# One fused attention and projection kernel: its projection stage written out without loops, the two parts of x cut by ScalarE and VectorE, SyncE led by events, and in the attention stage the attended lower part cut by VectorE with the residual sums first

## The chip, the core and the metric

The kernel runs on one core of a Trainium2 chip. The metric is the device time of one execution in microseconds (us), as a median over runs. The core has five engines with a queue each: TensorE (PE) multiplies matrices, VectorE (DVE), ScalarE (ACT) and GpSimd (POOL) work on elements, and SyncE (SP) issues transfers (DMA). They meet only at semaphores. A wait in a queue holds everything behind it in that queue.

## The reference

x has 2 sequences of 2048 rows of 1024. One attention layer with 32 query heads of 32 and a single key and value head, a residual sum with a layer norm, one product with a 1024x1024 weight (both operands scaled and clipped to 448 and scaled back), a second residual sum and layer norm.

```python
q = (x @ wq_w.T + wq_b).reshape(b, t, H, HD)        # H = 32, HD = 32
k = (x @ wk_w.T + wk_b).reshape(b, t, HKV, HD)      # HKV = 1
v = (x @ wv_w.T + wv_b).reshape(b, t, HKV, HD)
scores = jnp.einsum('bqhd,bkd->bhqk', q, k1) / jnp.sqrt(jnp.float32(HD))
weights = jax.nn.softmax(jnp.where(causal, scores, -jnp.inf), axis=-1)
attn = jnp.einsum('bhqk,bkd->bqhd', weights, v1).reshape(b, t, H * HD)
x1 = _layernorm(x + attn @ wo_w.T + wo_b)
x_sim = jnp.clip(x1 * x_scale, -448, 448)
w_sim = jnp.clip(weight * w_scale, -448, 448)
out = _layernorm(x1 + x_sim @ w_sim * (1.0 / (x_scale * w_scale)))
```

## The kernel before, in words

Every queue is written out by hand; there is no scheduler. A value that needs precision is held as an upper part (a cast to fp32r) and a lower part (the value less the upper part), and a product is made of three matmuls: upper by upper, lower by upper, upper by lower (`THREE`).

**Projection stage.** x comes transposed in TB = 8 blocks of 512 rows. For each block PE makes MT = 9 tiles: G = 8 units of queries (`project`, 24 matmuls each, into two PSUM banks in turn) and one tile of keys and values (`project_keys`, 16 matmuls, one bank for all blocks). `norm` sums squares after the fifth unit and after the keys. In the last block the keys come first; PE waits there for `raw_ready` of the block before, that is until ACT has copied the keys of that block out of their bank. For a unit ACT adds the bias (`raw`) and squares it (`sq`), DVE cuts `raw` into `part_hi` and `part_lo` (`cut_queries`), ACT stores both (`send`). `raw` and the parts have two buffers, so unit m of PE waits for the squares of unit m-2, and those for DVE's cut of unit m-2 before. For the keys ACT copies one part of the bank (`kv_sum`, L756), DVE adds the other (L963), ACT makes four copies with the bias (L759, L760).

The parts of x: `xt_raw` has one buffer in two halves, `xt_hi` and `xt_lo` have two buffers. In block 0 ACT makes `xt_hi` and DVE `xt_lo` by halves. From block 1 on POOL does both in `cut_x` (L644 cast, L646 subtraction), and behind each half adds the output bias to two row tiles of x (`add_bias_row`, L633), 32 in all, which SP loads from x and stores to `xb_d`. The 9 tiles of the projection weight are cut by DVE (L928, L931) before its first `cut_queries`. DVE also measures, and in blocks 4 to 7 clips, the 8 tiles of the second weight (`wf_tile`).

SP's queue is a loop over blocks: load half of x, wait for its landing, two row loads, two row stores (each waits for POOL), then the weight tile. After the loop come the last two pairs of rows, then the loads of the output weight `w_o` into `xt_raw` (L452), which ACT (`upper_wo`, L784) and DVE (`lower_wo`) cut during the last block. In the last block ACT's queue has, per unit: `add_bias`, `send` of the unit before, `upper_wo` of the unit before, and in four units squares of keys. DVE reduces key norms there (L1015), for which PE's `key_norm` (L1288) waits.

**Attention stage.** 544 steps; a step is one key tile of 128 against 16 heads of a query tile. PE makes scores (L1365), ACT the exponential (L838), DVE adds it into `acc` (L1117; the first addition of a group has the line L1113), PE weighs the values (L1377). Groups of steps end with `denominators` (L1387), `invert` on DVE, `spread_out` on PE (L1395) and `normalise_group` on DVE. Finished query tiles are cut into `att_hi` (ACT, L825) and `att_lo` (POOL, L689), multiplied with the output weight between scores (`half_projection`, L1350), and DVE adds the residual (`add_residual`, L1094) and takes moments. At which step each of these stands is set by `places`: a tile is cut at its step 4 or 13, and its product begins at 6 or 22.

**Last stage.** Loops over 32 row tiles with the second product. Nothing of it is touched.

## Time and profile before

| what | us |
|---|---|
| median of 3 runs (2452.33 to 2453.8) | 2452.48 |
| the profiled execution: its own time | 2451.5 |
| its span, first to last instruction | 2449.8 |
| PE busy in the span | 2347.4 |
| DVE busy in the span | 1859.7 |
| ACT busy in the span | 1319.6 |
| POOL busy in the span | 918.0 |

The granted TensorE clock has a mean of 0.988 of full speed. PE's projection runs from 13.28 to 438.82 us of the span, attention from 444.10. The duration of a matmul in the trace is longer than the distance from one to the next, since they overlap: in the projection 0.39 us and 0.227 us at full clock.

### The profile page before, as it was taken

Reading aid. Unit: us, or ns where it says so; the run is one execution under the profiler, and the core shown is the slowest. Engines: PE = TensorE matmul, PEld = TensorE weight load, DVE = VectorE, ACT = ScalarE, POOL = GpSimd, SP = SyncE. Lnnn points to the kernel's source line nnn. Section 1 sums busy time; section 2 is a strip of 40 time slices with the busy share of each in tenths; the row PEclk is TensorE's granted clock in tenths of the full one; section 3 lists DMA queues with packets and bytes.
Section 4 is the critical chain, followed back from the end, with each engine's and each line's share of the span. In section 5 each row is a group of like instructions: output and inputs, shape, how many; then the busy total and the mean of one; then the engine's idle time right before and its main releaser. Section 6 shows DMA issues by size and latency. Waiting matters only on the chain.

```text
span 2449.8 us, 35663 instructions
## 1 busy us (share of the span) xinstructions
PE 2347.4 (96%) x13933; PEld 1488.8 (61%) x13933; DVE 1859.7 (76%) x1387; ACT 1319.6 (54%) x1443; POOL 918.0 (37%) x472
## 2 busy tenths in 40 slices
PE   6999998789999999999999999999999998999998
PEld 5778776335555555555555555555555556888887
DVE  6655665788888888888889998888888886444444
ACT  2232224577777777777777676777777773100000
POOL 2553453013233233234232323332324323666563
PEclk9999999899999999999999999999999999999999
DMA  7775767231222112212221122212221212222221
GB/s 234 260 254 204 278 241 258 60 62 36 53 57 66 44 45 66 66 45 58 53 66 44 44 55 63 58 44 61 53 63 44 66 61 112 91 89 86 86 94 61
DMA packets 159958, 231.55 MB, mean 95 GB/s; under 512 B 9582, under 2 KB 109902, under 8 KB 157774
## 3 DMA queue, kind: packets, MB, share of 16 engines
q1 hardware_dynamic: 136206, 178.27, 25.1%
q10 hardware_dynamic: 23616, 51.39, 5.5%
q8 instruction: 94, 1.54, 0.3%
q14 instruction: 42, 0.34, 0.1%
HBM read 140.50 MB, written 89.13 MB: 94 GB/s over the span
## 4 chain that ended last, share of the span: by engine, by line
PE 64%; DVE 7%; ACT 5%; POOL 3%; issue 2%; DMA 0%; ACTq 0%; DVEq 0%; POOLq 0%
PE bank L1365 18%; PE bank L1377 16%; PE bank L1440 14%; PE bank L1350 12%; ACT prob L838 4%; DVE acc L1117 4%; POOL att_lo L689 2%; PE bank L1387 2%; PE bank L1430 1%; DVE acc L1113 1%; PE bank L1395 1%; POOL prob L684 1%; DVE r_den L1077 1%; ACT att_hi L825 1%; DVE r_hi L1079 0%
## 5 line engine op out<-in xcount | busy, mean ns | idle before, releaser
L838 ACT ACTIVATE prob<-bank 128x1024 f32<-128x1024 f32 x1088 | 1055.4, 1023 | 422.5 <-PE bank L1365 394.7
L1117 DVE TENSOR_TENSOR acc<-acc,prob 128x2048 f32<-128x2048 f32 x420 | 987.4, 2351 | 71.4 <-ACT prob L838 48.6
L1365 PE MATMUL bank<-q_st,keys 98*128 98x512 f32 x2176 | 646.8, 416 | 16.5 <-ACT prob L838 13.3
L1365 PEld LDWEIGHTS bank<-q_st,keys 98*128 98x128 f32 x2176 | 376.5, 189 | 352.9 <-ACT prob L838 258.4
L1377 PE MATMUL bank<-prob,v_t 128*32 128x512 f32 x4352 | 526.2, 601 | 0.0
L684 POOL TENSOR_SCALAR_AFFINE_SELECT prob<-prob 128x1024 f32<-128x1024 f32 x128 | 204.1, 1617 | 591.6 <-ACT prob L838 591.6
L1377 PEld LDWEIGHTS bank<-prob,v_t 128*32 128x32 f32 x4352 | 114.0, 109 | 263.4 <-issue 251.9
L1113 DVE TENSOR_TENSOR acc<-prob 128x2048 f32<-128x2048 f32 x60 | 141.5, 2358 | 118.5 <-ACT prob L838 78.7
L1259 PE MATMUL bank<-xt_hi,w_hi 128*128 128x512 f32 x512 | 204.8, 400 | 19.1 <-DVE xt_lo L921 15.3
L1350 PE MATMUL bank<-wo_hi,att_hi 128*128 128x512 f32 x512 | 209.1, 408 | 11.9 <-POOL att_lo L689 8.5
L869 ACT ACTIVATE xs_hi<-bank 128x1024 fp32r<-128x1024 f32 x32 | 32.9, 1027 | 336.3 <-DVE y L900 261.5
L689 POOL TENSOR_TENSOR att_lo<-att,att_hi 128x1024 fp32r<-128x1024 f32 x31 | 99.7, 3217 | 295.9 <-ACT att_hi L825 295.9
L621 POOL TENSOR_SCALAR moments<-moments 128x1 f32<-128x1 f32 x64 | 68.6, 1072 | 367.9 <-DVE moments L895 361.1
L1350 PE MATMUL bank<-wo_hi,att_lo 128*128 128x512 f32 x512 | 202.8, 396 | 0.0
L1440 PE MATMUL bank<-wf_hi,xs_hi 128*128 128x512 f32 x512 | 202.2, 395 | 0.7 <-DVE xs_lo L1189 0.7
L1350 PE MATMUL bank<-wo_lo,att_hi 128*128 128x512 f32 x512 | 202.5, 396 | 0.0
L1259 PE MATMUL bank<-xt_lo,w_hi 128*128 128x512 f32 x512 | 202.3, 395 | 0.0
L1259 PE MATMUL bank<-xt_hi,w_lo 128*128 128x512 f32 x512 | 202.2, 395 | 0.0
L1440 PE MATMUL bank<-wf_lo,xs_hi 128*128 128x512 f32 x512 | 199.7, 390 | 0.0
L1440 PE MATMUL bank<-wf_hi,xs_lo 128*128 128x512 f32 x512 | 199.3, 389 | 0.0
L766 ACT ACTIVATE raw<-bank,bias 128x512 f32<-128x512 f32 x64 | 44.1, 689 | 252.8 <-PE bank L1259 226.7
L953 DVE CAST part_hi<-raw 128x512 fp32r<-128x512 f32 x64 | 86.3, 1349 | 104.4 <-ACT raw L766 70.1
(132 smaller groups left out, 2643.2 us busy)
## 6 DMA issues: line engine op xcount, KB each, us to landing
q_st<-q_hi_d SPq DMA_DIRECT2D x128, 256.0 KB
xt_raw<-x_t SPq DMA_DIRECT2D x16, 1024.0 KB, 6.6
q_hi_d<-part_hi ACTq DMA_DIRECT2D x64, 256.0 KB, 2.7
q_lo_d<-part_lo ACTq DMA_DIRECT2D x64, 256.0 KB, 3.2
x_row<-x SPq DMA_DIRECT2D x32, 512.0 KB, 4.6
xb_d<-x_row SPq DMA_DIRECT2D x32, 512.0 KB, 2.7
q_st<-q_lo_d SPq DMA_DIRECT2D x64, 256.0 KB
res<-xb_d SPq DMA_DIRECT2D x32, 512.0 KB, 5.7
```

Of the source, the lines that this page charges most:

```text
L621: nc.gpsimd.tensor_scalar(moments[:, 1:2], moments[:, 1:2], LN_EPS, None, ALU.add).then_inc(done, 1)
L684: nc.gpsimd.affine_select(out=tri, in_=tri, compare_op=ALU.is_ge, fill=0.0, base=0, pattern=[[0, 2 * HG], [1, P]], channel_multiplier=-1). ...
L689: nc.gpsimd.tensor_tensor(att_lo[q % 2][:], att[:, q % TILES_KEPT], att_hi[q % 2][:].bitcast(F32), ALU.subtract).then_inc(att_cut, 1)
L838: nc.scalar.activation(prob[:, s % SLOTS, 2 * p:2 * p + 2], bank[:, 2 * p:2 * p + 2], ACT.Exp, scale=SCALE).then_inc(p_done, 1)
L953: nc.vector.tensor_copy(part_hi[:, m % 2], raw[:, m % 2]).then_inc(hi_cut, 1)
L1113: nc.vector.tensor_tensor(acc[:, n % 2], prob[:, (s - 1) % SLOTS], new, ALU.add).then_inc(acc_done, 2)
L1117: nc.vector.tensor_tensor(acc[:, n % 2], acc[:, n % 2], new, ALU.add).then_inc(acc_done, 1)
L1259: last = nc.tensor.matmul(dst, (w_hi, w_lo)[a][:, m, k], (xt_hi[:, r], xt_lo[r])[c][:, k], start=(k == 0 and a == c == 0), stop=(k == KT - ...
L1350: last = nc.tensor.matmul(dst, (att_hi, att_lo)[a][q % 2][:, k], (wo_hi, wo_lo)[c][:, k, cols], start=(at == 0), stop=(at == len(todo) - 1 ...
L1365: last = nc.tensor.matmul(bank[:, g].rearrange("p (a n) -> p a n", n=P), keys[:, k // QT, k % QT * P:(k % QT + 1) * P], queries[:, :, g], ...
L1377: last = nc.tensor.matmul(bank[g * HD:(g + 1) * HD, 4 + n % 2], v_t[:, k // QT, k % QT], prob[:, s % SLOTS, g], start=(t == 0), stop=(t == ...
L1440: last = nc.tensor.matmul(bank[:, 4 + 2 * (r % 2) + h], (xs_hi, xs_lo)[a][:, r % 2, k], (wf_hi, wf_lo)[c][:, k, cols], start=(k == 0 and a ...
```

## The change

SP, POOL, ACT and DVE have the projection stage written out without loops, and in PE blocks 0 and 1 are outside the loop (as blocks 6 and 7 were). Three functions of the block and the unit say where a piece of side work stands: `half_at` (halves of x), `row_at_unit` (row tiles), `tile_use` (tiles of the second weight).

- x of block 0 comes in four quarters, issued without a wait between them, with a semaphore each; ACT and DVE cut quarters, and PE's first unit waits for quarters. The four stores of zeros by ACT come behind its four casts.
- x of block b+1 is cut during block b: ACT casts a half (`upper_x`, 128x2048) and DVE subtracts (`lower_x`), at units 1 and 4 (5 and 7 in block 0). POOL has none of it.
- DVE adds the bias to the row tiles, one tile at each of five units in blocks 1 to 6, two in block 7. POOL has none of it.
- DVE cuts four weight tiles ahead of its first `cut_queries` and one tile ahead of each of the next five.
- SP waits for the event that frees a buffer at the place where it comes in DVE's order, and issues the loads of `w_o` behind row 29, ahead of the stores of rows 30 and 31.
- In the attention stage DVE makes `att_lo`, and at a step that has several pieces the residual sums stand ahead of `invert`, `normalise_group` and `att_lo`; the moments behind.

```diff
@@ SP
-            for half in range(2):
-                sp.dma_start(xt_raw[:, k], x_t[0, :, k]).then_inc(xt_in, 16)
-                sp.wait_ge(xt_in, 16 * (half + 1))
+            for quarter in range(4):
+                k = slice(quarter * KT // 4, (quarter + 1) * KT // 4)
+                sp.dma_start(xt_raw[:, k], x_t[0, :, k]).then_inc(xt0_in[quarter], 16)
             for m in range(1, MT):
                 load_w(m)
+                if m == 6:
+                    load_x(1, 0)
+                    load_x(1, 1)
...
+            for b in range(TB - 1):
+                for m in range(G):
+                    if half_at(b, m) is not None and b + 2 < TB:
+                        load_x(b + 2, half_at(b, m))
+                    if row_at_unit(b, m) is not None:
+                        next_row(row_at_unit(b, m))
+                    if tile_use(b, m) is not None:
+                        next_tile(tile_use(b, m))
@@ POOL
-                    nc.gpsimd.tensor_copy(xt_hi[:, r, k], xt_raw[:, k]).then_inc(xt_hi_cut, 1)
-                    nc.gpsimd.tensor_tensor(xt_lo[r][:, k], xt_raw[:, k], xt_hi[:, r, k].bitcast(F32), ALU.subtract).then_inc(xt_cut, 1)
-                nc.gpsimd.tensor_tensor(x_row[:, i], x_row[:, i], bo[:], ALU.add).then_inc(x_row_added, 1)
-                    nc.gpsimd.tensor_tensor(att_lo[q % 2][:], att[:, q % TILES_KEPT], att_hi[q % 2][:].bitcast(F32), ALU.subtract).then_inc(att_cut, 1)
@@ ACT
+            for tb in range(TB - 1):
                 for m in range(MT):
                     add_bias(tb, m, m)
                     if m >= 1:
                         send(tb, m - 1)
+                    if half_at(tb, m + 1) is not None:
+                        upper_x(tb + 1, half_at(tb, m + 1))
@@ DVE, projection
+            for tb in range(TB - 1):
+                for m in range(G):
+                    if tb == 0 and m + 4 < MT:
+                        cut_weight(m + 4)
+                    cut_queries(tb, m, m)
...
+                if half_at(tb, m) is not None:
+                    lower_x(tb + 1, half_at(tb, m))
+                if row_at_unit(tb, m) is not None:
+                    add_bias_row(row_at_unit(tb, m))
@@ DVE, attention
+                if s in sum0_at:
+                    add_residual(sum0_at[s], 0)
+                if s in sum1_at:
+                    add_residual(sum1_at[s], 1)
                 if s % 2 == 0 and s // 2 in group_of_den:
                     invert(group_of_den[s // 2])
                 if s % 2 == 0 and s // 2 - 1 in group_of_den:
                     normalise_group(group_of_den[s // 2 - 1])
-                if s in sum0_at:
-                    add_residual(sum0_at[s], 0)
+                if s in split_at:
+                    lower_attended(split_at[s])
```

The DVE queue in block 0, before: the last two weight tiles, then the first queries.

```order
L928 CAST w_hi<-w_stage 128x1024
L931 TENSOR_TENSOR w_lo<-w_stage,w_hi 128x1024
L928 CAST w_hi<-w_stage 128x1024
L933 TENSOR_TENSOR w_hi<-w_stage,w_hi 128x8x64
L990 UNCONDITIONAL_BRANCH
L990 ISA
L952 ISA
L953 CAST part_hi<-raw 128x512
L954 ISA
L955 TENSOR_TENSOR part_lo<-raw,part_hi 128x512
```

The same queue now, behind weight tile 3.

```order
L903 CAST w_hi<-w_stage 128x1024
L906 TENSOR_TENSOR w_lo<-w_stage,w_hi 128x1024
L951 CAST part_hi<-raw 128x512
L953 TENSOR_TENSOR part_lo<-raw,part_hi 128x512
L903 CAST w_hi<-w_stage 128x1024
L906 TENSOR_TENSOR w_lo<-w_stage,w_hi 128x1024
L951 CAST part_hi<-raw 128x512
L953 TENSOR_TENSOR part_lo<-raw,part_hi 128x512
```

The cut of the first queries moved from behind nine weight tiles to behind five.

SP's queue at the end of the projection, before (the L405 and L408 rows are the last two pairs of row tiles, L452 is the output weight).

```order
L405 DMA x_row<-x 128x1024 x2
L408 DMA xb_d<-x_row 128x1024 x2
L405 DMA x_row<-x 128x1024 x2
L408 DMA xb_d<-x_row 128x1024 x2
L452 DMA xt_raw<-w_o 128x1024 x4
```

The same place now.

```order
L438 DMA xb_d<-x_row 128x1024
L433 DMA x_row<-x 128x1024
L438 DMA xb_d<-x_row 128x1024
L433 DMA x_row<-x 128x1024
L465 DMA xt_raw<-w_o 128x1024 x4
L438 DMA xb_d<-x_row 128x1024 x2
```

The loads of the output weight passed the stores of the last two rows, and rows 0 to 29 are done by the end of block 6.

DVE's queue at one of the steps 4 of the attention stage, before (L1087 is `normalise_group`).

```order
L1117 TENSOR_TENSOR acc<-acc,prob 128x2048 x2
L1087 TENSOR_TENSOR att<-att,bank 128x512
L1094 TENSOR_TENSOR res<-bank,res 128x512
L893 BN_STATS stats<-res 128x6 x2
L895 BN_AGGR moments<-stats 128x2
L1117 TENSOR_TENSOR acc<-acc,prob 128x2048 x7
```

The same step now.

```order
L1118 TENSOR_TENSOR acc<-acc,prob 128x2048 x2
L1090 TENSOR_TENSOR res<-bank,res 128x512
L1083 TENSOR_TENSOR att<-att,bank 128x512
L1100 TENSOR_TENSOR att_lo<-att,att_hi 128x1024
L876 BN_STATS stats<-res 128x6 x2
L878 BN_AGGR moments<-stats 128x2
L1118 TENSOR_TENSOR acc<-acc,prob 128x2048 x7
```

The residual sum passed the normalisation, and the lower part stands between it and the moments.

## Rows read from the trace of the kernel before

**Rows 1.** Page part 1: busy us (share of the span) and instructions by engine.

```profile
PE 2347.4 (96%) x13933; PEld 1488.8 (61%) x13933; DVE 1859.7 (76%) x1387; ACT 1319.6 (54%) x1443; POOL 918.0 (37%) x472
```

**Rows 2.** Windows of PE: stretch, length, PE busy (x), granted clock, DMA share, GB/s.

```profile
13.28:76.01 62.73, 54.06 (x217) 0.94 0.68 232
76.01:125.55 49.54, 49.54 (x217) 0.97 0.74 264
125.55:173.84 48.29, 48.29 (x217) 1.00 0.76 273
...
366.98:375.29 8.31, 0.00 (x1) 0.81 0.60 236
375.29:438.82 63.53, 57.54 (x256) 0.94 0.71 241
```

**Rows 3.** Timeline of the start: start, us, engine, line, what, [idle before <-releaser].

```profile
8.99 1.91 ACT L742 ACTIVATE xt_hi<-xt_raw 128x2048 fp32r<-128x2048 f32 x1 [3.48 <-DMA xt_raw<-x_t]
10.93 2.29 DVE L921 TENSOR_TENSOR xt_lo<-xt_raw,xt_hi 128x2048 fp32r<-128x2048 f32 x1 [3.26 <-ACT xt_hi L742]
...
13.28 0.79 PE L1259 MATMUL bank<-xt_hi,w_hi 128*128 128x512 f32 x1 [13.28 <-DVE xt_lo L921]
...
20.16 0.50 PE L1259 MATMUL bank<-xt_hi,w_hi 128*128 128x512 f32 x1 [2.04 <-DVE xt_lo L921]
...
44.95 0.80 PE L1259 MATMUL bank<-xt_hi,w_hi 128*128 128x512 f32 x1 [3.82 <-ACT sq L768]
...
75.39 0.62 PE L1236 MATMUL bank<-sq,head_sum 128*32 128x512 bf16 x4 [2.81 <-ACT sq L768]
```

**Rows 4.** Tile w_stage: from the issue of a 512 KB load to its landing.

```profile
DMA to landing us min/median/max: 3.4/3.8/4.7
```

**Rows 5.** Timeline at the end of block 6, POOL, DVE and PE.

```profile
360.40 4.66 POOL L646 TENSOR_TENSOR xt_lo<-xt_raw,xt_hi 128x2048 fp32r<-128x2048 f32 x1
...
360.63 4.98 DVE L955 TENSOR_TENSOR part_lo<-raw,part_hi 128x512 fp32r<-128x512 f32 x1
...
370.79 0.68 DVE L937 TENSOR_REDUCE norms<-bank 128x512 f32 x1
371.39 0.67 DVE L963 TENSOR_TENSOR kv_sum<-bank,kv_sum 64x512 f32<-64x512 f32 x1
...
375.29 3.75 PE L1245 MATMUL bank<-xt_hi,w_hi 128*128 128x512 f32 x8 [8.31 <-issue]
```

**Rows 6.** Timeline of the last block: SP, ACT and PE.

```profile
396.30 2.25 SPq L452 DMA_DIRECT2D xt_raw<-w_o  x4
...
401.42 1.06 ACT L784 ACTIVATE wo_hi<-xt_raw 128x1024 fp32r<-128x1024 f32 x1 [8.28 <-DMA xt_raw<-w_o]
...
414.11 0.37 PE L1288 MATMUL bank<-kv_sum,head_sum 32*32 32x512 bf16 x1 [2.07 <-DVE norms L1015]
...
428.84 0.37 PE L1288 MATMUL bank<-kv_sum,head_sum 32*32 32x512 bf16 x1 [1.91 <-DVE norms L1015]
```

**Rows 7.** Attention stage, windows: stretch, length, busy of PE, PEld, DVE, ACT, POOL.

```profile
480.00:1960.00 1480.00, 1442.35 (x9680) 785.54 (x9680) 1293.67 (x864) 1076.89 (x1137) 472.68 (x235) 1.00 0.22 54
```

**Rows 8.** Lines of PE from 480 to 1960 us: busy, mean ns | idle before, releasers.

```profile
L1350 PE MATMUL bank<-wo_hi,att_hi 128*128 128x512 f32 x456 | 186.7, 409 | 11.9 <-POOL att_lo L689 8.5 <-DVE res L1094 3.1
...
L1387 PE MATMUL bank<-acc,head_col 128*32 128x128 f32 x1952 | 65.9, 276 | 7.8 <-DVE acc L1117 7.8
...
L1395 PE MATMUL bank<-r_parts,spread 128*128 128x128 f32 x240 | 35.4, 270 | 9.3 <-DVE r_parts L1081 9.2
```

**Rows 9.** Tile att_lo: duration ns min/median/max, first and last start.

```profile
L689 POOL TENSOR_TENSOR att_lo<-att,att_hi x31: 2374/3542/4021, 553.9 to 2021.1; 128x1024 fp32r<-128x1024 f32 x31
L1143 DVE TENSOR_TENSOR att_lo<-att,att_hi x1: 1224/1224/1224, 2037.0 to 2037.0; 128x1024 fp32r<-128x1024 f32 x1
```

**Rows 10.** Tile acc (min/median/max ns), then page part 5 (busy us, mean ns).

```profile
L1117 DVE TENSOR_TENSOR acc<-acc,prob x420: 2266/2292/4297, 452.3 to 2028.1; 128x2048 f32<-128x2048 f32 x140
...
L1117 DVE TENSOR_TENSOR acc<-acc,prob 128x2048 f32<-128x2048 f32 x420 | 987.4, 2351 | 71.4 <-ACT prob L838 48.6
```

**Rows 11.** Timeline at one step 4 of the attention stage.

```profile
1047.52 3.54 POOL L689 TENSOR_TENSOR att_lo<-att,att_hi 128x1024 fp32r<-128x1024 f32 x1 [11.00 <-ACT att_hi L825]
...
1048.74 0.68 DVE L1087 TENSOR_TENSOR att<-att,bank 128x512 f32<-128x512 f32 x1
```

More of the change, by code:

```diff
@@ L191, in build @@
         zeros_sent = sem("zeros_sent")
-        xt_in = sem("xt_in")
+        xt0_in = [sem(f"xt0_in{i}") for i in range(4)]
+        xt0_hi, xt0_cut = sem("xt0_hi"), sem("xt0_cut")
+        xt_in = [sem("xt_in0"), sem("xt_in1")]
         xt_hi_cut, xt_cut = sem("xt_hi_cut"), sem("xt_cut")
@@ L437, in _, with load_row @@
-            load_x(KT // 2, 0)
-            load_tile(KT - 1)
-            load_x(KT // 2, 1)
-            sp.wait_ge(wf_tile_read, KT + 1)
-            sp.dma_start(wf_tile[:], w_f[:, 0]).then_inc(wf_tile_in, 16)
-            with sp.Fori(KT // 2 + 1, TB) as tb:
-                for half in range(2):
-                    load_x(tb, half)
-                    store_piece(tb * 2 + (half - 2 - KT))
-                    load_piece(tb * 2 + (half - 1 - KT))
-            for pair in range(TILES // 2 - 2, TILES // 2):
-                add_bias_rows(pair)
+            def load_row(r):
+                sp.dma_start(x_row[:, r % 2], x_tiles[r]).then_inc(x_row_in[r % 2], 16)
@@ L733, in _ @@
                 act.sem_inc(s, 16)
+            for quarter in range(4):
+                k = slice(quarter * KT // 4, (quarter + 1) * KT // 4)
+                act.wait_ge(xt0_in[quarter], 16)
+                nc.scalar.activation(flat(xt_hi[:, 0, k]), flat(xt_raw[:, k]), ACT.Copy).then_inc(xt0_hi, 1)
             act.wait_ge(consts, 5)
@@ L738, in _ @@
                     act.dma_start(max_d[c].rearrange("t h n -> (t h) n")[i * P:(i + 1) * P], zeros).then_inc(zeros_sent, 16)
-            for half in range(2):
-                k = slice(half * KT // 2, (half + 1) * KT // 2)
-                act.wait_ge(xt_in, 16 * (half + 1))
-                nc.scalar.activation(flat(xt_hi[:, 0, k]), flat(xt_raw[:, k]), ACT.Copy).then_inc(xt_hi_cut, 1)
             act.wait_ge(b_in, 16)
@@ L768, in add_bias, with upper_x @@
                     nc.scalar.activation(sq[:, m % HG], bank[:, m % 2], ACT.Square, bias=bias[:, m:m + 1]).then_inc(sq_ready, 1)
-            with act.Fori(0, TB - 1) as tb:
+            def upper_x(tb, half):
+                k = slice(half * KT // 2, (half + 1) * KT // 2)
+                act.wait_ge(xt_in[half], 16 * tb)
+                nc.scalar.activation(flat(xt_hi[:, tb % 2, k]), flat(xt_raw[:, k]), ACT.Copy).then_inc(xt_hi_cut, 1)
+            for tb in range(TB - 1):
                 for m in range(MT):
@@ L967, in sum_keys @@
                 nc.vector.reduce_sum(centre_part[0:SR, bass.ds(tb, 1)], one(kv[0:SR, bass.ds(tb, 1)]), AX.X).then_inc(k_summed, 1)
-            def block_work(tb, use_tile):
-                for m in range(G):
-                    cut_queries(tb, m, m, use_tile)
-                norm(tb, 1)
-                add_lower_keys(tb)
-                sum_keys(tb, G)
             def weight_scale():
@@ L1141, in _ @@
             lower_wf(0)
[L1142 to L1143 removed]
+            lower_attended(LAST_B)
             for i in range(1, 4):
@@ L1255, in project @@
                 for k in range(KT):
-                    if k % (KT // 2) == 0:
+                    if first and k % 2 == 0:
+                        pe.wait_ge(xt0_cut, k // 2 + 1)
+                    elif not first and k % (KT // 2) == 0:
                         pe.wait_ge(xt_cut, tb * 2 + (2 + k // (KT // 2) + 1))
@@ L1261, in project, with project_block @@
                 last.then_inc(qkv_done, 1)
-            def project_block(tb, r):
+            def project_block(tb, r, first=False):
                 for m in range(G):
-                    project(tb, r, m)
+                    project(tb, r, m, first and m == 0)
                     if m == HG:
@@ L1269, in project_block @@
                 norm(tb, 1)
-            with pe.Fori(0, TB // 2 - 1) as i:
+            project_block(0, 0, first=True)
+            project_block(1, 1)
+            with pe.Fori(1, TB // 2 - 1) as i:
                 for r in range(2):
```

167 lines of the change are left out of this document (74 added, 93 removed).

## The prediction, written before the changed kernel ran

> **What bounds the kernel now.** I read the busy shares first: PE is busy 96% of the span, DVE 76%, ACT 54%, POOL 37% [rows 1]. So a gain has to come from PE: from time in which it stands still, or runs at its lower clock, or starts late. Then I cut PE's projection into blocks. Blocks 2 to 6 take 48.29 us each and PE is busy in all of it (one of the five is in [rows 2]): there the projection has nothing to give, and the loops that end inside this stretch cost PE nothing. Block 0 takes 62.73 us with 54.06 busy, the last block 63.53 with 57.54 busy, and between blocks 6 and 7 PE stands for 8.31 us [rows 2]. The timeline of the start says why: the first matmul waits until 13.28 for the lower part of half of x, then come gaps of 2.04, 3.82 and 2.81 us [rows 3]. In the attention stage PE is busy 1442.35 of 1480 us, DVE 1293.67, which is 87% [rows 7]; PE's idle 37.7 us are all that stage can give, and any DVE work added there meets an engine that is nearly full. One unit of 24 matmuls is 24 x 0.227 = 5.44 us; a block is 8 of these, 16 matmuls of keys (3.6) and two norms.
>
> **The start.** Now the first half of x lands at 8.99, ACT casts it in 1.91 and DVE subtracts in 2.29 [rows 3]: 8.99 + 1.91 + 2.29, with some 0.1 between, is 13.28. With quarters, ACT takes 1.06 (the same shape in [rows 6]) and DVE 1.22 [rows 9]. When the first quarter lands is not in the trace. It cannot be before 1.7 + 3.4 = 5.1 (issue behind the first weight tile, and the fastest landing of 512 KB [rows 4]) nor after 8.99. I take 6.3: it is nearer to the lower end since the zeros, 1 MB that shared the DMA engines, now go later. PE starts at 6.3 + 1.06 + 1.22 = 8.6 (bounds 7.5 and 11.3). Gain 4.7 us (2.0 to 5.8).
>
> The quarters then follow each other at intervals that I estimate at 1.5 us (the engine steps are 1.06 and 1.22), while PE at half clock needs 6 x 0.45 = 2.7 us for a quarter, so the gap of 2.04 has no successor.
>
> **Blocks 0 and 1.** Block 0 lost 62.73 - 48.29 = 14.4 us: gaps 8.67, and 54.06 - 48.29 = 5.8 of matmuls at the lower level, 1.2 GHz (mean granted clock 0.94 [rows 2]); block 1 takes 49.54 and adds 1.3. These 7.1 us belong to four stretches, at the start and behind each gap: 1.8 us each. The 3.82 gap exists because DVE cuts all nine weight tiles before the first queries, so ACT has no free `raw`; the 2.81 gap because DVE's queries stood behind stretched operations beside POOL. After the change a weight tile is 0.69 + 1.23 of DVE work per unit of 5.44 us and is loaded at a rate of one per load and cut, at most 4.7 + 1.9 = 6.6 us for a buffer, two buffers, so 3.3 us a tile: faster than PE uses them. What is left is the low clock of the start itself, 1.8 us. Gain 14.4 + 1.3 - 1.8 = 13.9 us (bounds 8, if one of the later gaps survives with its clock loss, and 15.7).
>
> **What moves onto ACT and DVE.** 14 halves of x: ACT 14 x 1.91 = 27 us, DVE 14 x 2.29 = 32 us [rows 3]. 32 row tiles on DVE: this form is not in the trace for DVE; between 1.22 (same size, subtraction [rows 9]) and twice that, I take 1.22, so 39 us. Per unit DVE then has 1.1 for the queries, at most 2.29 or 1.22 + 1.5 beside, under 4.5 of 5.44 us: hidden behind PE. Cover goes if a row tile is not there when DVE waits for it, for the queries stand behind this wait, then ACT, then PE. A row's load follows the landing of the store two rows earlier, 2 x 4.7 us at most by [rows 4] against two units of 10.9 us; and `raw` has two buffers, which gives one more unit. I cost it at 0, with an upper bound of 5 us.
>
> **Between blocks 6 and 7.** PE waits for ACT's copies of the keys, and those for DVE's sum, which begins at 371.39, since its queries were stretched: a `part_lo` that takes 0.69 us elsewhere takes 4.98 beside POOL's subtraction of 4.66 [rows 5]. From the end of that sum to PE's start it is 375.29 - 372.06 = 3.2 us of ACT. With DVE free at 366.98 it needs 0.68 for the norm and 0.67 for the sum: 366.98 + 1.4 + 3.2 = 371.6, a gap of 4.6 us instead of 8.31. Gain 3.7 us (0 to 4.3). The clock drops all the same, as it did after 2.81 us.
>
> The Trainium skill, SBUF — State Buffer, "SBUF: two separate sides", says that VectorE and GpSimd share one port pair as an exclusive lock, and whoever comes second waits for the whole instruction of the other. The 4.98 us are 0.3 us more than POOL's own 4.66, so the trace agrees here.
>
> **The last block.** Against 8 x 5.44 + 3.6 and some 4.8 of norms, transposes and key norms, 51.9 us, it takes 63.5: 6.0 of gaps, 5.6 of low clock. The first cause is ACT: its queue stands 8.28 us on the output weight that SP issues only at 396.30, behind four row tiles [rows 6]. All units after it come late, DVE with them, and PE waits 2.07 and 1.91 for key norms. In the new order SP issues these loads behind row 29, about 20 us before ACT's first use of them, so they land (5 us, from 396.30 to 401.42) ahead of need. What is late next are the key norms themselves: DVE has about 5.0 to 6.3 us of work in units 3 to 6 against 5.44, so I leave 1.5 us of waits, and 1.8 of low clock behind the boundary gap: 55.2 us. Gain 8.3 us (3 to 9.8). At the end of the stage DVE comes out of unit 6 about 1 us late for the flag: loss 0.9.
>
> **Attention.** DVE gets 31 x 1.22 = 38 us [rows 9]. It loses what POOL did to it: the additions have a mean of 2351 against a median of 2292 ns, 420 x 0.059 = 25 us [rows 10], plus about 6 in other forms. The net is some +7 us on an engine with 186 us of idle, so the bound stays PE. On the path: at a step 4, POOL delivers at 1047.52 + 3.54 = 1051.06; DVE begins its side work at 1048.74 [rows 11] and has 0.6 + 0.6 + 1.22 ahead of the end of `att_lo`: 1051.2. Equal, so the 8.5 us of PE waiting for `att_lo` [rows 8] stay, under another name. At a step 13 the stretched addition (up to 4.3 instead of 2.3) is replaced by 1.22 us, so groups that end soon after are 0.4 to 0.8 us earlier: of the 7.8 us of waits for `acc` and the 9.3 for `r_parts` I take 5 back. Residual sums first: saves perhaps 1 of the 3.1 for `res`, and costs up to 0.6 at each of about 15 steps where `invert` now stands behind it; I charge 3. Net gain 3 us (bounds -10 and +12).
>
> The lock rule named above would make each of the 31 subtractions hold DVE for its full median 3.54 us, 110 us in all, and moving them would free 110 - 38 = 72 us of DVE. The additions show 25, so the rule alone overstates it here: at the steps 4 it is POOL that is stretched and DVE keeps its 2.29. The sum goes by the 25.
>
> **Sum.** 4.7 + 13.9 + 3.7 + 8.3 - 0.9 + 3 = 32.7 us, of which 29.7 before the attention stage. The profiled execution took 2451.5 (span 2449.8), so 2418.8; the median of the runs is 1.0 above it: 2420 us.
>
> **Rivals.** (a) Half of the projection's gain: new waits take the place of the old. For it: the DMA share is already 0.7 [rows 2], and SP's queue is now a chain of store, wait, load, so one late store delays x or `w_o`. Against it: x is loaded a block ahead. Then 2451.5 - 15 - 3 + 1 = 2434. (b) DVE in the attention stage becomes the bound, the slower side. Place: steps 4 of each pair, and denominators after a step 13. Price: if none of the 38 us are covered and nothing comes back from POOL, -29.7 + 38, 8 us more than now, so 2461; it decides from the point at which each of the 31 subtractions exposes more than 29.7 / 31 = 0.96 us on PE. For it 87% busy; against it that `prob` has four buffers (`SLOTS`), so ACT's exponential of a step needs the addition of four steps earlier, and a late one is not noticed at once. (c) Attention gives more: waits for `acc`, `r_parts` and `res` go by 12 us, not 3, and the start is at its early bound, 1 us more: 2410. (d) The change does not do what it says: PE's first unit waits for the fourth quarter in effect, or the boundary wait is unmoved since it hangs on ACT; then the first term or the third is zero, 2424 or 2425. This lies within my range.
>
> **How the numbers follow.** The forecast, with (d) inside, has 0.70 and its own range is 2412 to 2428. (a) has 0.14, (c) 0.12, (b) 0.04. The range of 2410 to 2434 holds the forecast, most of (c) and half of (a). Faster or slower begin at 0.2%, 5 us, about what a measurement of this kernel can tell from no change. All cases but (b) are faster; for what I have not thought of I leave a little: faster 0.93, within 3%, slower 4%.
>
> **What would show it.** First matmul between 7.5 and 11.3, block 0 under 51 us, and the later gaps of block 0 gone: the start is right. `part_lo` at 0.69 us throughout and a gap of 4 to 5 us ahead of the last block: the boundary. The output weight issued ahead of the last block, no ACT wait on it, and the last block at 54 to 57 us: the third term. In attention the additions at 2.3 us with waits for `att_lo` about as before. I am wrong if PE in blocks 1 to 6 is no longer busy throughout (a row tile or a half of x came late), or if the waits in the attention stage exceed 45 us.

## The result and the profile after

| | median us | lowest to highest | runs |
|---|---|---|---|
| before | 2452.40 | 2449.0 to 2453.8 | 4 |
| after | 2417.06 | 2413.82 to 2417.97 | 4 |

The ratio is 0.9853 with a 95% interval of 0.9835 to 0.9870: 35.3 us faster. The profiled execution of after has a span of 2411.7 us against 2449.8, so 38.1 us less, which is what the terms below are taken from. (It is the fastest of the four executions of after; the spans of the other three are 2414.3 to 2415.9.) PE's first score matmul starts at 417.83 instead of 444.10: 26.3 us come from the projection stage, 11.8 from behind it.

The busy times of the engines after, against [rows 1]:

```profile
PE 2338.3 (97%) x13933; PEld 1484.1 (62%) x13933; DVE 1809.0 (75%) x1466; ACT 1346.0 (56%) x1459; POOL 640.1 (27%) x381
```

POOL lost 278 us of work. ACT gained 26 for its 14 halves of x. DVE took over subtractions, row tiles and `att_lo` and is nevertheless 51 us less busy: what it had lost to stretching was more than what it was given. The clearest form is this one, which had a mean of 1349 ns before:

```profile
L951 DVE CAST part_hi<-raw 128x512 fp32r<-128x512 f32 x64 | 28.3, 443 | 140.6 <-ACT raw L741 121.7
```

PE's windows after, with the columns of [rows 2]: blocks 0 and 1, the gap ahead of the last block, the last block, and the tail up to the first scores.

```profile
9.23:59.32 50.09, 50.09 (x217) 1.00 0.78 288
59.32:107.60 48.28, 48.28 (x220) 1.00 0.71 250
349.04:353.57 4.53, 0.07 (x4) 0.72 0.60 172
353.57:411.20 57.63, 55.76 (x256) 0.96 0.66 228
411.20:417.83 6.63, 0.59 (x4) 0.60 0.29 108
```

Block 0 has no gap left and costs 1.8 us more than a full-speed block; blocks 1 and 2 are at the 48.29 that was the floor (48.28 and 48.29). The gap is 4.5 us instead of 8.3, the last block 57.6 instead of 63.5, still with 1.87 us idle inside: the waits for key norms are 0.5 us (4.4 before), and 1.4 us are one wait for ACT's squares, which before had too.

The start after (same columns as [rows 3]):

```profile
1.74 2.03 SPq L413 DMA_DIRECT2D xt_raw<-x_t  x4
...
6.70 1.06 ACT L713 ACTIVATE xt_hi<-xt_raw 128x1024 fp32r<-128x1024 f32 x1 [3.99 <-DMA xt_raw<-x_t]
7.79 2.54 DVE L914 TENSOR_TENSOR xt_lo<-xt_raw,xt_hi 128x1024 fp32r<-128x1024 f32 x2 [0.25 <-ACT xt_hi L713]
...
9.23 0.77 PE L1264 MATMUL bank<-xt_hi,w_hi 128*128 128x512 f32 x1 [9.23 <-DVE xt_lo L914]
```

And the end of block 6, against [rows 5]: the lower part takes 0.69 us (4.98 before), the norm and the sum of the keys follow the bank at once, and the wait of PE is ACT's 3 us of copies with little ahead of them. SP issues the output weight at 357.31 (396.30 in [rows 6]).

```profile
346.34 0.69 DVE L953 TENSOR_TENSOR part_lo<-raw,part_hi 128x512 fp32r<-128x512 f32 x1
...
349.16 0.69 DVE L935 TENSOR_REDUCE norms<-bank 128x1 f32<-128x512 f32 x1 [0.99 <-PE bank L1239]
...
350.47 2.21 ACT L734 ACTIVATE kv<-kv_sum,bias 32x512 f32<-32x512 f32 x3 [1.07 <-DVE kv_sum L965]
...
353.57 3.75 PE L1248 MATMUL bank<-xt_hi,w_hi 128*128 128x512 f32 x8 [4.47 <-issue]
357.31 2.01 SPq L465 DMA_DIRECT2D xt_raw<-w_o  x4
```

In the attention stage, first the window with the columns of [rows 7]; it begins the same distance behind the first scores as the window of before did:

```profile
453.70:1933.70 1480.00, 1452.90 (x9744) 791.69 (x9744) 1302.27 (x900) 1085.36 (x1146) 378.49 (x206) 1.00 0.22 55
```

PE is idle for 27.1 us of it, not 37.7. PE's lines from 453 to 1933 us, against [rows 8], show which waits went:

```profile
L1357 PE MATMUL bank<-wo_hi,att_hi 128*128 128x512 f32 x462 | 189.0, 409 | 14.4 <-issue 11.3 <-DVE res L1090 3.1
...
L1394 PE MATMUL bank<-acc,head_col 128*32 128x128 f32 x1952 | 65.9, 276 | 0.2
L1402 PE MATMUL bank<-r_parts,spread 128*128 128x128 f32 x244 | 35.6, 268 | 4.5 <-DVE r_parts L1077 4.2
```

The denominators wait 0.2 us instead of 7.8, the spread ones 4.5 instead of 9.3; the product with the output weight waits 14.4 instead of 11.9. "issue" there is the wait for `att_lo`, for which the profile found no releaser; the last experiment shows it. The additions and `att_lo`, against [rows 9, 10]: minimum, median and maximum in ns.

```profile
L1118 DVE TENSOR_TENSOR acc<-acc,prob x420: 2266/2292/2295, 426.0 to 1989.6; 128x2048 f32<-128x2048 f32 x140
```
```profile
L1100 DVE TENSOR_TENSOR att_lo<-att,att_hi x32: 1217/1218/2118, 529.5 to 1998.5; 128x1024 fp32r<-128x1024 f32 x32
```

No addition is stretched any more (the longest was 4297). The 2118 of `att_lo` and the 1075 below are not free of POOL: both stand behind its masking of `prob`, which the last section takes up.

```profile
L1077 DVE SCALAR_TENSOR_TENSOR r_parts<-r_hi,r_lower,r_den x64: 350/352/1075, 475.7 to 1994.4; 128x128 fp32r<-128x128 f32 x64
```

How did a stretched addition reach PE? Of the 8.0 us that PE of before waited for `acc` in all, 7.2 us are six waits of 1.1 to 1.4 us, and all six look like this one:

```profile
975.82 3.94 POOL L689 TENSOR_TENSOR att_lo<-att,att_hi 128x1024 fp32r<-128x1024 f32 x1 [5.87 <-ACT att_hi L825]
977.61 4.30 DVE L1117 TENSOR_TENSOR acc<-acc,prob 128x2048 f32<-128x2048 f32 x1
...
984.51 4.24 POOL L684 TENSOR_SCALAR_AFFINE_SELECT prob<-prob 128x1024 f32<-128x1024 f32 x2 [4.75 <-ACT prob L838]
984.81 2.99 DVE L1117 TENSOR_TENSOR acc<-acc,prob 128x2048 f32<-128x2048 f32 x1
...
987.95 1.08 PE L1387 MATMUL bank<-acc,head_col 128*32 128x128 f32 x32 [1.11 <-DVE acc L1117]
```

The subtraction on POOL stretches one addition by 1.6 to 2.0 us. DVE is late by that much, so that a later addition begins 0.3 to 0.4 us behind POOL's masking instead of ahead of it and is stretched by another 0.7, and this is the addition for which `denominators` waits. In after all 54 additions that overlap a masking began ahead of it, in `attention_only` below, whose edit touches nothing but the attention stage, all 55, and none took more than 2295 ns.

### The profile page after: what moved, and what is told of

The parts are those of the page before. It is cut to its first block, busy times and chain, and to the rows that moved or that the text cites. A ratio compares the mean times of both kernels' runs of the same rounds, so it can differ in the third digit from the quotient of the medians.

```text
span 2411.7 us, 34838 instructions
## 1 busy us (share of the span) xinstructions
PE 2338.3 (97%) x13933; PEld 1484.1 (62%) x13933; DVE 1809.0 (75%) x1466; ACT 1346.0 (56%) x1459; POOL 640.1 (27%) x381
## 4 chain that ended last, share of the span: by engine, by line
PE 71%; DVE 5%; ACT 3%; issue 2%; POOL 1%; DMA 0%; ACTq 0%; DVEq 0%; POOLq 0%
PE bank L1372 20%; PE bank L1384 18%; PE bank L1447 14%; PE bank L1357 13%; ACT prob L821 3%; DVE acc L1118 2%; PE bank L1394 2%; POOL prob L663 1%; PE bank L1437 1%; PE bank L1402 1%; DVE acc L1114 1%; DVE r_den L1073 1%; DVE r_parts L1077 0%; DVE res L1090 0%; DMA wf<-wf_sim_d 0%
## 5 line engine op out<-in xcount | busy, mean ns | idle before, releaser
L1118 DVE TENSOR_TENSOR acc<-acc,prob 128x2048 f32<-128x2048 f32 x420 | 961.1, 2288 | 58.1 <-ACT prob L821 35.1
L1372 PE MATMUL bank<-q_st,keys 98*128 98x512 f32 x2176 | 646.8, 416 | 16.6 <-ACT prob L821 13.2
L663 POOL TENSOR_SCALAR_AFFINE_SELECT prob<-prob 128x1024 f32<-128x1024 f32 x128 | 206.4, 1636 | 743.2 <-ACT prob L821 743.2
L1357 PE MATMUL bank<-wo_hi,att_hi 128*128 128x512 f32 x512 | 209.0, 408 | 14.4 <-issue 11.3
L951 DVE CAST part_hi<-raw 128x512 fp32r<-128x512 f32 x64 | 28.3, 443 | 140.6 <-ACT raw L741 121.7
L1357 PEld LDWEIGHTS bank<-wo_hi,att_hi 128*128 128x128 f32 x512 | 96.2, 188 | 47.8 <-issue 30.0
```

What stands on the lines that cost most here:

```text
L663: nc.gpsimd.affine_select(out=tri, in_=tri, compare_op=ALU.is_ge, fill=0.0, base=0, pattern=[[0, 2 * HG], [1, P]], channel_multiplier=-1). ...
L1118: nc.vector.tensor_tensor(acc[:, n % 2], acc[:, n % 2], new, ALU.add).then_inc(acc_done, 1)
L1357: last = nc.tensor.matmul(dst, (att_hi, att_lo)[a][q % 2][:, k], (wo_hi, wo_lo)[c][:, k, cols], start=(at == 0), stop=(at == len(todo) - 1 ...
L1372: last = nc.tensor.matmul(bank[:, g].rearrange("p (a n) -> p a n", n=P), keys[:, k // QT, k % QT * P:(k % QT + 1) * P], queries[:, :, g], ...
```

## The experiments

Theory A is the account that the profile after suggests: the terms of projection and attention are separate and add up; in attention DVE on its own is faster than DVE with POOL beside it, and the new order of the sums is worth nothing (the prediction had charged it 2 to 3 us). The rivals differ by experiment and stand in the texts. Four kernels ran on one chip (before there: median 2453.23, 2447.96 to 2455.9, 9 runs), four on another (2451.53, 2448.53 to 2454.51, 9 runs). Where a kernel has a single run, only places inside the trace are compared closely; its total is good to a few us.

### The change in two halves

`attention_only` is the kernel before with nothing but this:

```diff
-                if s in split_at:
-                    q = split_at[s]
-                    pool.wait_ge(att_hi_cut, q + 1)
-                    nc.gpsimd.tensor_tensor(att_lo[q % 2][:], att[:, q % TILES_KEPT], att_hi[q % 2][:].bitcast(F32), ALU.subtract).then_inc(att_cut, 1)
...
+                if s in sum0_at:
+                    add_residual(sum0_at[s], 0)
+                if s in sum1_at:
+                    add_residual(sum1_at[s], 1)
                 if s % 2 == 0 and s // 2 in group_of_den:
                     invert(group_of_den[s // 2])
...
+                if s in split_at:
+                    lower_attended(split_at[s])
```

> The kernel before with the attention part of the change alone: VectorE makes the attended lower part, residual sums first; the projection stage is as before. Theory (GpSimd's subtraction had stretched VectorE's additions ahead of the group ends): the attention stage gets 10 to 12 us shorter than before and the projection stays, so 2440 to 2443 us; waits for acc (7.8 us) go to under 1, those for r_parts fall from 9.3 to about 4.5. Rival (the attention stage gained because the projection ended differently, with other traffic or another clock): no change, 2450 to 2453.

`projection_only` is the kernel after with these attention lines put back as they were before.

> The changed kernel with the attention part as before: GpSimd makes the attended lower part, residual sums last. Theory: the first score matmul of the attention stage at 417 to 419 us of the span as in the changed kernel, the rest as before, so 26 us faster than before, 2425 to 2428 us. Rival as above: the attention stage keeps its gain, 2415 to 2418.

| kernel | median us (range, runs) | ratio to before, 95% | span | first to last exponential, starts |
|---|---|---|---|---|
| attention_only | 2439.89 (2436.11 to 2442.14, 6) | 0.9950 (0.9935 to 0.9966) | 2436.7 | 1565.3 |
| projection_only | 2426.93 (2425.68 to 2428.61, 4) | 0.9901 (0.9880 to 0.9921) | 2424.6 | 1577.8 |
| before | 2453.23 | | 2449.8 | 1578.5 |
| after | 2417.06 | 0.9853 | 2411.7 | 1566.4 |

By spans the halves give 13.1 and 25.2 us, together 38.3, and the whole gave 38.1. By medians they give 13.3 and 26.3, together 39.6, against 36.2 for the whole (2453.23 less 2417.06); the intervals are 4 to 5 us wide to each side for each, so both fit. One source of such differences can be seen: from the last exponential to the end, where nothing was edited, before and after take 425.8 and 426.2 us and `projection_only` 428.5. The length of the attention stage is the closer measure: 13.2 us less than before in `attention_only`, 12.1 in after, 0.7 in `projection_only`. The attention term comes from an edit of some ten lines. PE's waits there (us in total, times, longest), first `attention_only`, then `projection_only`:

```profile
PE bank L1354 <- issue: 11.3, 15, 0.8
...
PE bank L1399 <- DVE r_parts L1077: 3.9, 9, 0.8
```
```profile
PE bank L1403 <- DVE r_parts L1081: 9.2, 14, 1.3
PE bank L1358 <- POOL att_lo L668: 8.5, 11, 0.9
PE bank L1395 <- DVE acc L1122: 8.0, 8, 1.4
```

With POOL's subtraction the waits are those of before to the tenth, and the longest addition is again 4297 ns; without it there is no wait for `acc`, and that for `r_parts` is less than half. Nothing of the projection is needed for that.

### Which part of the attention edit: the order of the sums

`sums_last` is after, with the residual sums again behind `invert`, `normalise_group` and `att_lo`:

```diff
-                if s in sum0_at:
-                    add_residual(sum0_at[s], 0)
-                if s in sum1_at:
-                    add_residual(sum1_at[s], 1)
...
                 if s in split_at:
                     lower_attended(split_at[s])
+                if s in sum0_at:
+                    add_residual(sum0_at[s], 0)
                 if s in sum1_at:
                     q = sum1_at[s]
+                    add_residual(q, 1)
```

> The changed kernel with the residual sums behind invert, normalise_group and the attended lower part; VectorE still makes the lower part. Theory A (the sums first were worth about nothing, since they delay invert by 0.6 us at some 15 steps and save as much for the lower part's reader): within 3 us of the changed kernel, 2414 to 2420, and with the lower part 0.6 us earlier at the steps 4 its waits fall from 11 to about 3 us while the waits for res rise. Rival B (the sums first are what took the waits for r_parts away): r_parts back at 9 us, 2421 to 2424.

Measured: 2415.24 us (2414.71 to 2416.06, 4 runs), ratio to before 0.9851 (0.9831 to 0.9871), the same as after; the attention stage lasts 1566.1 us against 1566.4. PE's waits:

```profile
PE bank L1356 <- DVE res L1090: 15.2, 18, 1.1
...
PE bank L1401 <- DVE r_parts L1077: 2.8, 7, 0.8
...
PE bank L1393 <- DVE acc L1118: 1.3, 2, 1.1
```

The 11.3 us on `att_lo` and 3.1 on `res` are now 15.2 on `res` alone. At such a step PE needs both the lower part and the bank whose sum DVE reads, so the order on DVE only says which of the two is named. Sums first is worth nothing that can be measured; the 12 to 13 us are the move off POOL. (The wait of 1.1 us for `acc` follows an addition of 3229 ns, the one that here began behind a masking and was stretched.)

### Is it POOL's presence as such: the bias rows back on POOL

`rows_on_pool` leaves `add_bias_row` to POOL, each one behind DVE's cast of the same unit, and the rest as after:

```diff
+            for b in range(TB // 2):
+                for m in range(G):
+                    if row_at_unit(b, m) is not None:
+                        pool.wait_ge(hi_cut, b * G + m + 1)
+                        add_bias_row(row_at_unit(b, m))
```

> The changed kernel with the bias additions to the 32 row tiles by GpSimd, each behind VectorE's cast of the same unit; x stays with ScalarE and VectorE. Theory (GpSimd's two-input additions hold VectorE's queries, and slack of a unit hides it inside blocks): part_lo or part_hi stretched to 2 to 3 us in the 32 units concerned, PE still busy throughout blocks 1 to 6, and the gap ahead of the last block grows from 4.5 to 5 to 7 us, since row 29 stands at the last unit of block 6; total 0 to 4 us slower than the changed kernel. Rival (it was the larger subtractions of x alone that hurt): gap of 4.5 us, no difference.

Measured: 2417.3 us (1 run), span 2415.6, the gap ahead of the last block 4.47 as in after. The expectation of stretched queries failed: `part_lo` is at 691 to 695 ns in the whole projection. The figures are those of the rival (no difference), but its reason, that only the larger subtractions hurt, isn't shown by them. DVE and POOL in block 6:

```profile
341.07 0.69 DVE L967 TENSOR_TENSOR part_lo<-raw,part_hi 128x512 fp32r<-128x512 f32 x1
341.12 2.90 POOL L647 TENSOR_TENSOR x_row<-x_row,bo 128x1024 f32<-128x1024 f32 x1 [2.54 <-DVE part_hi L965]
341.68 2.89 DVE L957 TENSOR_SCALAR wf_tile<-wf_tile,small 128x1024 f32<-128x1024 f32 x1
```

`part_lo` began 0.05 us ahead of POOL and kept its 0.69 us; the scaling that began 0.56 us behind POOL's start took 2.89 instead of the 0.75 it takes in after. So an overlap is needed, with DVE second, and here it fell on an operation for which nobody waits. This is one placement of the row additions, behind DVE's cast of each unit; before had others, where `part_hi` and `part_lo` were stretched beside row additions too. No run puts the cutting of x alone back on POOL. Where DVE's operation is on the path, as `part_lo` at 360.63 in [rows 5], the same overlap costs PE time. The Trainium skill, SBUF — State Buffer, "SBUF: two separate sides", has VectorE and GpSimd exclude each other for the length of an instruction. These rows agree with that for the scaling: from its start to POOL's end it is 2.34 us, and it grew by 2.14.

### The order in block 0, and the issue of the output weight

`weights_first` cuts all nine weight tiles ahead of the first queries, as before did:

```diff
-            for m in range(1, 4):
+            for m in range(1, MT):
                 cut_weight(m)
...
-                    if tb == 0 and m + 4 < MT:
-                        cut_weight(m + 4)
```

> The changed kernel with all nine weight tiles cut by VectorE ahead of its first queries, as before. Theory (it was this order that made the gap of 3.82 us in block 0): PE reaches its fifth unit at about 33 us and stands there until VectorE's first queries behind the last weight tile, at 38 to 44 us, since the 2 MB of the next block of x now travel ahead of the last two weight tiles: one gap of 6 to 12 us and 1.8 us of low clock, block 0 at 58 to 64 us instead of 50.1; 8 to 14 us slower, 2424 to 2431. Rival (the gap was made by GpSimd's port alone): block 0 stays under 52 us.

Measured: 2423.61 us (1 run), span 2421.5, so 6.5 us more than after's median and 9.8 by span: the low end of what was expected, or just below it. The last block begins 10.5 us later than in after (364.03 against 353.57). PE and DVE:

```profile
40.74 0.76 PE L1262 MATMUL bank<-xt_hi,w_hi 128*128 128x512 f32 x1 [6.52 <-issue]
```
```profile
34.07 0.69 DVE L903 CAST w_hi<-w_stage 128x1024 fp32r<-128x1024 f32 x1 [5.39 <-DMA w_stage<-w_qkv]
```

DVE stands 5.39 us on the landing of the last weight tile but one and cuts the first queries only at 37.27; ACT has no free `raw`, PE no free bank. That one gap of 6.5 us, and the lower clock around it (0.72 granted from 34.22 to 46.50), make most of the 10.5 us; the rest I did not separate. It isn't the gap of before over again: SP issues 2 MB of x ahead of the last two weight tiles now, so these land later than they did. In the new queues the order of the cuts is worth 10.5 us; how much of the 13.9 us of blocks 0 and 1 it carries by itself, against SP's order and POOL's absence, no run separates.

`late_wo` issues the first four loads of the output weight behind the last rows and the first sends of the last block, at 377.28 instead of 357.31:

```diff
+            next_row(TILES - 2)
+            next_row(TILES - 1)
+            for i in range(2):
+                sp.wait_ge(xb_sent[i], 16 * (TILES // 2))
+            sp.wait_ge(part_sent[0], 32 * ((TB - 1) * G // 2 + 2))
             sp.wait_ge(xt_cut, 2 * TB + 2)
             for k in range(4):
                 sp.dma_start(wo_stage[:, k], w_o[:, k]).then_inc(wo_in[k], 16)
-            next_row(TILES - 2)
-            next_row(TILES - 1)
```

> The changed kernel with the first four loads of the output weight behind the stores of rows 30 and 31 and behind the first stored queries of the last block, at about 376 us of the span instead of 357. Theory (ScalarE's stand on the output weight delayed the units of the last block): ACT waits 7 to 10 us ahead of its first wo_hi, PE stands 2 to 6 us more in the last block, which takes 60 to 64 us instead of 57.6; 3 to 6 us slower than the changed kernel. Rival (the slack of two units hides it and the gain of the last block came from VectorE's freedom alone): last block under 59 us.

Measured: 2418.01 us (1 run), span 2415.9. The total missed the expected 3 to 6 us: it is 1.0 above after's median, which one run can't tell from nothing. The last block is as expected, 61.0 instead of 57.6 us. ACT's wait and one of PE's two in [rows 6] are back:

```profile
380.82 1.06 ACT L770 ACTIVATE wo_hi<-xt_raw 128x1024 fp32r<-128x1024 f32 x1 [8.52 <-DMA xt_raw<-w_o]
```
```profile
393.48 0.37 PE L1298 MATMUL bank<-kv_sum,head_sum 32*32 32x512 bf16 x1 [2.04 <-DVE norms L1014]
```

ACT stands 8.5 us on one load, and PE's waits for key norms are 2.8 us in all, against 0.5 in after and 4.4 before. The block gives back 3.4 of the 5.9 us that it had gained; 2.3 of them are these waits, the other 1.1 I can't assign.

`quarters_waited` has SP wait for each quarter of x before it issues the next:

```diff
             for quarter in range(4):
                 k = slice(quarter * KT // 4, (quarter + 1) * KT // 4)
                 sp.dma_start(xt_raw[:, k], x_t[0, :, k]).then_inc(xt0_in[quarter], 16)
+                sp.wait_ge(xt0_in[quarter], 16)
```

> The changed kernel with a wait of SyncE for each quarter of x before it issues the next load. Theory (issue without waits is what closes the gap of the first unit): the first matmul at 9.2 us as now, the quarters 3.5 to 4 us apart, PE standing about 1 us ahead of each of three quarters, first unit done at 20 to 22 us instead of 16.8, block 0 4 to 6 us longer. Rival (finer pieces alone do it): unit done by 18 us.

Measured: 2421.99 us (1 run), span 2419.9, so 4.9 us more than after's median and 8.2 by span; the last block begins 9.2 us late, where 4 to 6 were expected. The direction was right, the size under-forecast:

```profile
16.25 0.50 PE L1265 MATMUL bank<-xt_hi,w_hi 128*128 128x512 f32 x1 [1.26 <-DVE xt_lo L915]
...
19.87 0.50 PE L1265 MATMUL bank<-xt_hi,w_hi 128*128 128x512 f32 x1 [1.96 <-DVE xt_lo L915]
...
23.94 0.80 PE L1265 MATMUL bank<-xt_hi,w_hi 128*128 128x512 f32 x1 [2.00 <-DVE w_lo L907]
```

The start of the first matmul doesn't depend on it (9.38 against 9.23), the three quarters behind it do, and I had forgotten the weight tiles that SP issues after them: the second unit waits 2.00 us for one. These gaps are 5.2 us, a fourth is 0.41, and the lower clock that follows them is most of the rest: from 12 to 30 us the mean granted clock is 0.81, in after it is at full speed from 13.13 on.

### A faster version

`combined` is after with three edits that its profile suggests. The last block begins with a unit of queries instead of the keys, so PE has 5.4 us of work while ACT copies the keys of block 6; `att_lo` stands right behind the residual sums, ahead of `invert` and `normalise_group`; one `lower_wo` moves behind the flag.

```diff
-            project_keys(TB - 1, 1)
             for m in range(G):
                 project(TB - 1, 1, m)
+                if m == 0:
+                    project_keys(TB - 1, 1)
...
+                if s in split_at:
+                    lower_attended(split_at[s])
                 if s % 2 == 0 and s // 2 in group_of_den:
                     invert(group_of_den[s // 2])
                 if s % 2 == 0 and s // 2 - 1 in group_of_den:
                     normalise_group(group_of_den[s // 2 - 1])
-                if s in split_at:
-                    lower_attended(split_at[s])
...
+            lower_wo(G - 3)
             lower_wo(G - 2)
             lower_wo(KT - 1)
```

> The changed kernel with three more moves: in the last block PE makes unit 0 ahead of the keys (ACT and DVE follow); at the steps of the attention stage VectorE makes the attended lower part right behind the residual sums, ahead of invert and normalise_group; the cut of output weight tile 5 goes behind the flag. Theory: the gap of 4.5 us ahead of the last block goes, with its 1.8 us of low clock: 6.3 us; the waits of 11.3 us at the steps 4 go to 1 to 4 us while those for r_parts grow by up to 2: 6 to 9 us; the flag comes 1.2 us earlier. Together 13 to 16 us faster than the changed kernel, 2401 to 2404. Rival (the waits at the steps 4 hang on the Y bank's sum or on att_hi, not on the lower part): half of the second term, 2406 to 2409.

Measured: 2405.89 us (2403.28 to 2411.84, 5 runs), ratio to before 0.9817 (0.9801 to 0.9832): faster than both, by 46 us than before and by 11 than after, and 2 us outside the expected 2401 to 2404. The first scores start at 409.96, 7.9 us earlier than in after. The attention stage lasts 1564.1 us, only 2.3 less. PE's waits:

```profile
PE bank L1407 <- DVE r_parts L1081: 8.3, 10, 1.3
...
PE bank L1399 <- DVE acc L1122: 3.8, 3, 1.6
PE bank L1362 <- issue: 2.6, 11, 0.2
...
PE bank L1362 <- DVE res L1094: 2.4, 4, 1.1
```

The nameless wait fell from 11.3 to 2.6 us by an edit that does nothing but move `att_lo` forward, so it was the wait for `att_lo`. `res` fell by 0.7. In exchange `invert`, now 1.22 us later, makes PE wait 4.1 us more for `r_parts`. The 3.6 more for `acc` have another cause, the one of before: three additions (2873, 3217 and 2926 ns) began just behind a masking on POOL, and PE's three waits for `acc` stand right behind them. One of the three:

```profile
1117.16 4.18 POOL L663 TENSOR_SCALAR_AFFINE_SELECT prob<-prob 128x1024 f32<-128x1024 f32 x2
1117.18 3.22 DVE L1122 TENSOR_TENSOR acc<-acc,prob 128x2048 f32<-128x2048 f32 x1
...
1120.54 1.08 PE L1399 MATMUL bank<-acc,head_col 128*32 128x128 f32 x32 [1.59 <-DVE acc L1122]
```

So 9.4 us are gained and 7.7 given back. The expectation had counted the first and up to 2 of the second.

## Why the prediction was right, and where it was off

| term | predicted | spans show |
|---|---|---|
| start, first matmul | 4.7 (2.0 to 5.8) | 13.28 - 9.23 = 4.05 |
| blocks 0 and 1 | 13.9 (8 to 15.7) | 12.64 + 1.26 = 13.9 |
| work moved onto ACT and DVE | 0 | 0: blocks 1 and 2 busy throughout |
| gap between blocks 6 and 7 | 3.7 (0 to 4.3) | 3.84 |
| last block | 8.3 (3 to 9.8) | 5.9 |
| tail | -0.9 | -1.35 |
| attention and behind | 3 (-10 to 12) | 11.8 |
| sum | 32.7 | 38.1 |

The time of 2417 lies in the forecast's own range, 3 us below the 2420. The mechanisms of the projection were right, and for block 0, the quarters and the last block a run shows that undoing them brings waits back; two sizes were wrong, with opposite signs. That the total came so close owes something to luck: attention gave four times its 3 us, the last block 2.4 less than its 8.3.

**Start.** The first cast began at 6.70, against 6.3 assumed. The other 0.2 is that PE saw `xt_lo` somewhat later than the 1.22 behind it. The quarters fed PE without a gap, as forecast, because all four are issued at once.

**Blocks 0 and 1.** The size is as forecast. `weights_first` shows that the new order of the weight tiles is needed (10.5 us without it); the part of the 2.81 gap that was put down to POOL is argued and not tested.

**Work moved over.** `part_lo` is at 691 to 695 ns in all of the projection, the row tiles took 1.22 us on DVE, the lower of the two bounds. DVE waited 3.6 us for two row tiles; none of it reached PE.

**Boundary.** Gap 4.47 against 4.6 forecast. What is left of it was ACT's three copies and the order on PE; `combined` starts with queries and has no gap there. How much of the 3.84 is POOL's work stays partly open: `attention_only`, with the projection of before, has 6.6 here and not 8.31, so this gap varies between executions by nearly half of the gain, and `rows_on_pool` did not bring it back.

```profile
PE bank L1249 <- issue: 6.6, 1, 6.6
```

**Last block, mis-sized.** The term that failed is the 51.9 us of work. What the lower clock costs can be read from windows, as length times the share of the clock that wasn't granted. These three have PE's columns as in [rows 2], the first from after, the others from before:

```profile
353.57:359.00 5.43, 5.43 (x15) 0.60 0.90 335
```
```profile
375.29:381.00 5.71, 5.71 (x17) 0.67 0.92 298
...
429.00:435.00 6.00, 5.78 (x18) 0.72 0.40 150
```

In after it is 5.43 x 0.40 = 2.2 us, so the work is 55.76 less 2.2, 53.6: the "some 4.8 of norms, transposes and key norms" was 1.7 too small. The trace before had this already: 1.9 and 1.7 us of low clock, not the "5.6", and 57.54 less 3.6, 53.9 of work. The forecast had taken 2 us of work for lost clock and counted on their return. The waits came out 1.87 against 1.5, though not as key norms (0.5) but for ACT's squares (1.4). The cause given for the waits before is right at least in part: of the 3.9 us of key-norm waits that went, `late_wo` brings 2.3 back.

**Attention, mis-sized.** The step that failed is "of the 7.8 us of waits for `acc` and the 9.3 for `r_parts` I take 5 back", with "I charge 3" for the sums. Measured: 7.6 and 4.8 came back, 12.4 us; the product with the output weight waits 2.5 more, close to the charge, though not by its reason, as `sums_last` shows. The waits account for 9.9 of the 11.8; the other 1.9 I cannot assign. I had read the stretching right (the additions' maximum fell from 4297 to 2295 ns) but priced it as a shift of 0.4 to 0.8 us for the groups that end soon after. What I missed is the second stretch: the late DVE came behind POOL's masking at the addition just ahead of `denominators`, and each of these six cost PE 1.1 to 1.4 us. Rival (c) had the size, 12 us. The term for `att_lo` was also off: its wait was to stay at 8.5 us and is 11.3. Of rival (b), the slower side, nothing came: DVE at 88% of the window makes PE wait less than the same engine at 87% with POOL beside it. Rivals (a) and (d) are out: the projection gave 26.3 of 29.7 us, and neither the start nor the boundary term was zero.

**What the stretching cost DVE.** The additions' busy time fell from 987.4 [rows 10] to 961.1, by 26.3 us, against the 25 of the forecast. The Trainium skill, SBUF — State Buffer, "SBUF: two separate sides", has the one that starts first keep the port pair and the other wait. The forecast worked 110 us out of that by taking POOL to be first all 31 times. The trace before agrees with the page and not with that reading: 22 additions began ahead of a subtraction on POOL that they overlap and took 2294 ns at most, 14 began behind one and took 3.0 to 4.3 us.

```profile
L1118 DVE TENSOR_TENSOR acc<-acc,prob 128x2048 f32<-128x2048 f32 x420 | 961.1, 2288 | 58.1 <-ACT prob L821 35.1
```

## What to carry to other kernels

When POOL does a large two-input operation beside a DVE that is nearly full, look at the maximum of DVE's forms, not only at their mean, and follow each stretched operation to the next point where PE waits for DVE: a few of them, and the delays that they cause in turn, can be worth more than their place in the sum suggests (here 12 us against 3), and giving the work to the busier engine can shorten both. Where PE waits in a step for several products of one engine, changing their order on that engine moves the wait from one name to another (0 us for the sums, 1.7 net for `att_lo`). In a hand-written queue, put the side work that waits for a DMA behind the work that PE needs: five tiles cut too early delayed the last block by 10.5 us here, and loads issued too late made it 3.4 longer.

## What the runs showed of the hardware that was not expected

In these traces the engine that begins second is the one that is stretched, beside POOL's masking of `prob` as beside its subtractions. The masking takes 1.1 us at its shortest and up to 3.2 where an addition began ahead of it, a mean of 1636 ns in after:

```profile
L663 POOL TENSOR_SCALAR_AFFINE_SELECT prob<-prob 128x1024 f32<-128x1024 f32 x128 | 206.4, 1636 | 743.2 <-ACT prob L821 743.2
```

All operations of DVE that are stretched in the attention stage of after began behind a masking: five `r_parts` of 350 ns took up to 1075, three `r_hi` of 226 ns up to 1018, and two `att_lo` 2.1 us instead of 1.2. In `combined` three additions that began so took 2.9 to 3.2 us. That no addition of after is among them is due to their order in time (54 overlap a masking, and all 54 began first), and an edit that moves DVE by a microsecond, as `combined` does, can end it.

The lower clock costs PE about 2 us at a time on top of the gap: block 0 of after, with that of the start alone, takes 50.09 us instead of 48.29, and the gap of 4.47 us is followed by the 2.2 us of the window above. Not every gap has it. In before a lower stretch comes with the gaps of 2.04, 3.82, 2.81 and 8.31 us, in them or within a microsecond behind, but the one of 2.07 us that ends at 414.11 is followed by full clock, and so is that of 2.04 us in `late_wo`:

```profile
411.00:417.00 6.00, 3.70 (x19) 1.00 0.79 260
```

Four transfers of 512 KB that are issued together land closer to one another than when each is waited for: the casts of the four quarters begin at 6.70, 8.02, 9.51 and 10.75 when issued at once (1.2 to 1.5 us apart), and at 6.60, 10.32, 13.88 and 17.50 when each is waited for (3.6 to 3.7 apart).
